# Exponentials and side counts one turn away from VectorE's work on them, in a fused attention and feed-forward kernel with a top-64 softmax

## What is computed

```python
q, k, v = (x @ W reshaped to 16 heads of 64)      # k and v get 4 memory rows in front
dots = einsum('bhid,bhjd->bhij', l2norm(q), l2norm(k)) * 10
dots = einsum('hg,bgij->bhij', W_pre_th, dots)     # mix the heads
dots = where(causal, -max, dots)
vk = top_k(dots, 64)[0][..., -1:]
attn = softmax(where(dots < vk, -max, dots))       # keep the 64 largest of a row
attn = einsum('hg,bgij->bhij', W_post_th, attn)    # mix the heads again
out = (attn @ v) * head_scale * sigmoid(x @ Wg + bg)
out = out @ Wo
```

## Time and profile before

| | |
|---|---|
| median of 3 runs | 3655.68 us (3652.28 to 3657.66) |
| the profiled execution's own time | 3655.08 us |
| span of its profile, first to last instruction | 3653.3 us |
| busy: PE, DVE, ACT, POOL | 2599.6, 1887.3, 1875.9, 1442.4 us |
| share of the span | 71%, 52%, 51%, 39% |
| mean granted TensorE clock | 0.795 of 2.4 GHz |

### The profile page before, as it was taken

The page is one execution under the profiler, slowest core; times in us unless marked ns, Lnnn a source line. Parts: engine busy times, 40 slices in busy tenths (PEclk is TensorE's granted clock), DMA queues, the critical chain, the costliest instruction groups (busy, mean ns, idle before and its releaser), DMA issues. The chain is left out here.

```text
span 3653.3 us, 58885 instructions
## 1 busy us (share of the span) xinstructions
PE 2599.6 (71%) x16099; PEld 1681.3 (46%) x16100; DVE 1887.3 (52%) x7291; ACT 1875.9 (51%) x6078; POOL 1442.4 (39%) x3918
## 2 busy tenths in 40 slices
PE   1985777777777776767677777676777777766498
PEld 1433444544454445544454445443544455444333
DVE  4262555545563556355545555455645563567335
ACT  1433555555654555455545554556545554565143
POOL 2003544444344444454444444544444335443000
PEclk9997777777877777877787777778877877787599
DMA  3001011001010111011101010011001010111101
GB/s 112 0 17 42 19 33 45 10 22 34 22 26 19 29 36 28 16 28 39 26 13 31 23 44 11 22 34 45 10 22 33 20 28 16 28 38 26 54 0 46
DMA packets 112976, 104.77 MB, mean 29 GB/s; under 512 B 34192, under 2 KB 110608, under 8 KB 112656
## 3 DMA queue, kind: packets, MB, share of 16 engines
q1 hardware_dynamic: 107744, 96.64, 10.4%
q10 hardware_dynamic: 4912, 4.46, 0.4%
HBM read 19.13 MB, written 12.71 MB: 9 GB/s over the span
## 5 line engine op out<-in xcount | busy, mean ns | idle before, releaser
L1395 DVE SCALAR_TENSOR_TENSOR E<-S,limit,E 128x68 f32<-128x68 f32 (+56 forms) x456 | 248.8, 579 | 1099.9 <-ACT E L1077 1074.3
L859 PE MATMUL bankC<-R,E 128*128 128x128 f32 x2560 | 475.4, 340 | 414.7 <-POOL R L1228 414.4
L859 PEld LDWEIGHTS bankC<-R,E 128*128 128x128 f32 x2560 | 415.0, 240 | 523.5 <-POOL R L1228 500.4
L1087 ACT COPY PT<-bankC 128x512 f32<-128x512 f32 (+3 forms) x512 | 216.5, 424 | 594.4 <-PE bankC L859 586.3
L1217 POOL TENSOR_SCALAR est<-below 128x1 f32<-128x1 f32 x456 | 93.2, 205 | 1029.0 <-ACT junk L1061 1007.7
L835 PE MATMUL bankD<-KT,QT 64*64 64x258 f32 (+7 forms) x2304 | 236.1, 485 | 353.2 <-ACT SC L1036 319.4
L845 PE MATMUL bankB<-raw,mixpre 128*128 128x76 f32 (+37 forms) x1024 | 417.7, 497 | 6.3 <-DMA raw<-SC 5.4
L1069 ACT ACTIVATE junk<-S 128x68 bf16<-128x68 f32 (+56 forms) x456 | 199.7, 439 | 432.3 <-DVE S L1333 432.0
L884 PE MATMUL bankM<-PT,V 128*64 128x64 f32 x5120 | 311.7, 292 | 0.8 <-ACT PTtail L1092 0.8
L845 PEld LDWEIGHTS bankB<-raw,mixpre 128*128 128x128 f32 x1024 | 187.6, 220 | 207.0 <-issue 188.0
L1189 POOL TENSOR_TENSOR S<-S,diagmask 128x8 f32<-128x8 f32 x512 | 127.3, 255 | 389.8 <-ACT S L1050 324.2
(11 more groups left out here) (173 smaller groups left out, 5428.5 us busy)
## 6 DMA issues: line engine op xcount, KB each, us to landing
X_first<-in_L_attn_x_dram ACTq DMA_DIRECT2D x8, 512.0 KB, 10.1
x<-X_first SPq DMA_DIRECT2D x8, 512.0 KB, 4.7
xt<-x SPq DMA_DIRECT2D x32, 128.0 KB, 3.2
x<-xt SPq DMA_DIRECT2D x32, 128.0 KB, 2.5
X_last<-x SPq DMA_DIRECT2D x8, 512.0 KB, 6.7
out_dram<-X_last SPq DMA_DIRECT2D x8, 512.0 KB, 3.2
raw<-SC SPq DMA_DIRECT2D x8, 258.0 KB, 4.5
raw<-SC SPq DMA_DIRECT2D x8, 254.0 KB, 4.1
```

The lines of the kernel that those rows point to most:

```text
L859: last = nc.tensor.matmul(bankC[n % 2][:, jb * P:(jb + 1) * P], E[n % 4][:, jb * P:(jb + 1) * P], R[n % 2][:, :], start=True, stop=True)
L1087: last = nc.scalar.copy(PT[u % 2][:, 0:blocks, :, at:at + IG], bankC[n % 2][:, 0:blocks * P].rearrange("p (j h i) -> p j h i", h=H, i=IG))
L1395: at[n] = step(nc.vector.scalar_tensor_tensor(out=E[n % 4][:, 0:w], in0=S[n % SBUFS][:, 0:w], scalar=least, in1=E[n % 4][:, 0:w], op0=ALU. ...
```

## The change

What moves: exp and count_sides of a pair both stand in ACT turn p+4 (before: turns p+6 and p+2), side counts first, and both behind the second evict of the turn; the two out_PT now follow each other. The waits of ACT are adapted. On POOL nmax comes first in the turn, then scaled_mix, then second_threshold. DVE shifts and takes the maxima of the pair four groups ahead instead of two, after the second round of 8 largest instead of between the rounds; the first four maxima are taken before the loop; ln_stats moves one turn earlier, and the squares of k one turn later. Instructions and buffers are the same in number and size.

```diff
--- before.py
+++ after.py
@@ -1043,6 +1043,8 @@
                 if is_ranked(n):
                     if ranked_upto(n - 2):
                         act.wait_ge(below_done, ranked_upto(n - 2))
+                    if ranked_upto(n - 6):
+                        act.wait_ge(signs_done, ranked_upto(n - 6))
                     nc.scalar.activation(junk[n % 2][:, 0:wide(n)], src, ACT.Square, scale=wide(n) ** -0.5,
                                          accum_out=msq[:, col(n)]).then_inc(summed, 1)
                     if is_wide(n):
@@ -1054,8 +1056,8 @@
 
             def count_below(n):
                 act.wait_ge(thr0_ready, ranked_upto(n))
-                if ranked_upto(n - 2):
-                    act.wait_ge(signs_done, ranked_upto(n - 2))
+                if ranked_upto(n - 4):
+                    act.wait_ge(signs_done, ranked_upto(n - 4))
                 act.wait_ge(summed, ranked_upto(n))
                 w = group_width(n)
                 nc.scalar.activation(junk[n % 2][:, 0:w], S[n % SBUFS][:, 0:w], ACT.Sign, scale=-1.0,
@@ -1063,8 +1065,10 @@
 
             def count_sides(n):
                 act.wait_ge(shifted, ranked_upto(n))
-                act.wait_ge(summed, ranked_upto(min(n + 2, NG - 1)))
-                act.wait_ge(below_done, ranked_upto(n))
+                if ranked_upto(n - 2):
+                    act.wait_ge(signs_done, ranked_upto(n - 2))
+                act.wait_ge(summed, ranked_upto(min(n + 4, NG - 1)))
+                act.wait_ge(below_done, ranked_upto(min(n + 2, NG - 1)))
                 w = group_width(n)
                 nc.scalar.activation(junk[n % 2][:, 0:w], S[n % SBUFS][:, 0:w], ACT.Sign,
                                      accum_out=signs[:, col(n)]).then_inc(signs_done, 1)
@@ -1126,16 +1130,15 @@
                         score(2 * t + 2, 1)
                     if g == 14 and ahead:
                         score(2 * t + 2, 3)
-                for n in (n0 - 6, n0 - 5):
+                if live:
+                    evict(n0 + 1)
+                for n in ranked_in(n0 - 4):
+                    count_sides(n)
+                for n in (n0 - 4, n0 - 3):
                     if 0 <= n < NG:
                         exp(n)
-                if live:
-                    evict(n0 + 1)
                 if n0 >= LAG:
                     out_PT(n0 - LAG)
-                for n in ranked_in(n0 - 2):
-                    count_sides(n)
-                if n0 >= LAG:
                     out_PT(n0 + 1 - LAG)
                 if live:
                     if g == 0 and ahead:
@@ -1236,21 +1239,21 @@
             for n0 in range(0, NG + LAG, 2):
                 t, g = divmod(n0, GPT)
                 live, ahead = n0 < NG, t + 1 < NT
-                if ranked_in(n0 - 2):
-                    second_threshold(ranked_in(n0 - 2))
+                if 0 <= n0 - 4 < NG:
+                    m = n0 - 4
+                    pool.wait_ge(max_done, m + 2)
+                    nc.gpsimd.tensor_scalar(nmax[:, ring((m, m + 1))], rmax[:, ring((m, m + 1))], -1.0, 1.0, ALU.mult,
+                                            ALU.mult).then_inc(nmax_ready, 2)
                 if n0 >= LAG:
                     scaled_mix(n0 - LAG)
                     scaled_mix(n0 + 1 - LAG)
+                if ranked_in(n0 - 2):
+                    second_threshold(ranked_in(n0 - 2))
                 if live:
                     mask(n0)
                     mask(n0 + 1)
                     if ranked_in(n0):
                         first_threshold(ranked_in(n0))
-                if 0 <= n0 - 4 < NG:
-                    m = n0 - 4
-                    pool.wait_ge(max_done, m + 2)
-                    nc.gpsimd.tensor_scalar(nmax[:, ring((m, m + 1))], rmax[:, ring((m, m + 1))], -1.0, 1.0, ALU.mult,
-                                            ALU.mult).then_inc(nmax_ready, 2)
                 for m in (n0 - 4, n0 - 3):
                     if 0 <= m < NG and m % GPB < 4:
                         if m >= 4:
@@ -1358,8 +1361,6 @@
                     for n in ranked:
                         dve.wait_ge(tk, at[n])
                         at[n] = step(nc.vector.max(top[n % 2][:, 0:8], near[n % 2][:, 0:group_width(n)]))
-                for n in ranked_in(n0 + 2):
-                    shift(n)
                 for r in range(1, WINDOW // 8):
                     for n in ranked:
                         row = near[n % 2][:, 0:group_width(n)]
@@ -1369,8 +1370,10 @@
                     for n in ranked:
                         dve.wait_ge(tk, at[n])
                         at[n] = step(nc.vector.max(top[n % 2][:, 8 * r:8 * r + 8], near[n % 2][:, 0:group_width(n)]))
-                if n0 + 2 < NG:
-                    for n in (n0 + 2, n0 + 3):
+                for n in ranked_in(n0 + 4):
+                    shift(n)
+                if n0 + 4 < NG:
+                    for n in (n0 + 4, n0 + 5):
                         row_max(n, ranked_upto(n))
                 if ranked:
                     for n in ranked:
@@ -1416,13 +1419,13 @@
             squares(0, 1)
             ln_stats(1)
             ln_apply(1)
-            for n in range(2):
+            for n in range(4):
                 row_max(n, 0)
             squares(1, 0)
             squares(1, 1)
             for n0 in range(0, NG, 2):
                 t, g = divmod(n0, GPT)
-                if g == 6 and t + 2 < NT:
+                if g == 4 and t + 2 < NT:
                     ln_stats(t + 2)
                 select_pair(n0)
                 if g == 4 and t:
@@ -1436,8 +1439,8 @@
                     if t + 2 < NT:
                         squares(t + 2, 0)
                     gate_half(2 * t)
-                if g == 14 and t + 2 < NT:
-                    squares(t + 2, 1)
+                if g == 0 and t and t + 1 < NT:
+                    squares(t + 1, 1)
                 if (n0 + 2) % GPB == 0:
                     mark_batch(n0 // GPB)
             gate_half(NU - 1)
```

## The result

The changed kernel takes 3053.23 us (median of 4 runs, 3052.16 to 3055.15) where the one before takes 3654.57: ratio 0.8355, 95% interval 0.834 to 0.8369. That is 601 us less, against a forecast of 380, and under the range's low end of 3140. The profiled execution took 3052.43 us, its span is 3050.7.

What follows compares the result with a forecast made beforehand. Bound: DVE and ACT waiting for each other, PE behind them. A tile of 80.8 + 21.7 = 102.5 us, for 116.2, scaled to 380 us off the attention: 3655.1 to 3275 us, range 3140 to 3500.

Steps and rivals of the forecast that it cites:

- The ring is opened: DVE and ACT wait for each other, 11.36 us a turn; becomes a two-turn loop, neither waiting in a plain turn.
- PE's wait for R: PE waiting for POOL's R at L859, 414.4 us before: should fall to the turns g = 8, under 200 us.
- I apply this share to the attention as a whole: 0.445 of one tile's PE idle time goes; applied to the attention's 860.6 us: 383 us, less 3 at the start.
- rival C: The clock rises too: busy PE shrinks by 216 us, two thirds of it on the path, 3131 us; chance 0.12.
- A: The attention as summed, with the waits of DVE and ACT opened: 3275 us, own range 3150 to 3420; chance 0.54.
- B: The ring is replaced by one through POOL (counts below, thr, shift, mask E, R, turn): 3515 us; chance 0.24.
- Handoffs at 1.3 us a turn: PE and ACT alternating over bankD and turned/out_PT: one 1.3 us handoff in each of seven turns, together 80.8 us.
- The turn g = 8: Turn with attend: R at 5.5 us, norm 1.1 us later, tail 16.0; 21.7 us for 22.44, bounds 20.2 and 22.4.
- waits and moves that cost nothing: ACT's new waits, POOL's nmax first, ln_stats earlier: covered or hidden; only the early maxima cost 3 us, once.
- Rival D: Exp stands behind both turn calls in ACT while R stays late: slower by 130 us, 3785; chance 0.05.
- exp behind turned: In ACT, exp waits for PE turn calls behind attend or project: 0.5 us in turns g = 0, 8 and 12.
- PE's wait for bankD: PE waiting until ACT has emptied bankD, 319.4 us before the change: should shrink least.

Runs made afterwards that it cites:

- the first experiment: Idle-time matmuls added ahead of the first turn call in turns g = 8: 14 on the kernel before, 3503.14 us; 10 on the kernel after, 2946.70 us.
- Q: POOL's new order (nmax, R, then second threshold): alone on the kernel before, 3470.97 us; the kernel after with it undone, 3583.01 us.
- X: Exponentials a turn earlier, behind the second evict: alone on the kernel before, 3699.41 us; the kernel after with it undone, 3042.22 us.
- a_norm8: The kernel after, with POOL's normalisation of k moved from the end of its turn g = 6 to the end of g = 8: 2933.93 us.

## Why the prediction was wrong

**The ring is opened: right in kind and in size.** I said PE would be left some 480 us idle in the attention; it is 482.9. ACT's wait before the side counts is gone, DVE waits at the shift, ACT's new wait at exp came as named; PE's wait for R, 210.7 us, stayed just over the 200 that I had set. That the idle time came out so close is partly luck: the share that goes was taken from one tile as 0.445, and it is 15.1 of 30.8, or 0.49, in that tile and 368 of 850.7, or 0.43, in the attention.

**The step that failed** is the one on which the sum was made: "I apply this share to the attention as a whole", with PE's busy time left at what it was, 85.4 us in the tile and 2177.8 overall. It fell by 228 us, to 1946.0. With the 368 of idle time that is 596 of the 601 us; the sum had put the busy time's part at nothing, without a price. I had that mechanism as rival C at 0.12, as another way to go, instead of a second term of the same sum. The sign for C, busy PE shrinking by more than 100 us, came, and the signs for A came with it.

C put the shrinking at 216 us for a clock of 0.90 and let two thirds of it count; it was 228 at 0.85, and all 228 stand beside the idle time in the 596. That C's 144 is near the 151 of the first experiment is chance, since these lie in the turns g = 8 and the gain of the change in the others. My argument against C, that a turn full of attend has the lowest clock and keeps it, was true of the change, at 0.60 before and after, but says nothing of the other turns, where the lower level went. Nor does that turn have to keep it: attend ran at 292 ns with a wait of 6 to 7 us ahead of it, and at 242 once that was filled. The Trainium skill says (TensorE: Matmul & The Clock Gate, "What's actually happening") that activity releases the throttle; the first experiment agrees with it.

One reading under C was wrong. The turn with 0.91 in the earlier trace rows is not one in which PE hardly waited: it was idle for 4.3 of 12.5 us. The turns g = 12 and g = 6 there, with 0.3 and 0.7 us idle, have 0.74 and 0.67. The clock of a turn does not follow from PE's idle time in the same turn. Under B, DVE is busy 9.3 to 10.2 us at g = 2 and 8 only, and 9.07 and 5.52 at g = 4 and 6.

**Handoffs at 1.3 us a turn** held as a sum in this tile. The seven turns took 71.8 us instead of 80.8, but the larger busy time of each is now 7.43, 8.36, 10.86, 9.86, 8.24, 9.37 and 7.68, together 61.8 instead of 71.7. That leaves 10.0 us for seven turns, 1.4 each. But the single turns leave from 0.3 to 2.8 us, so it is a mean and not one handoff in each. What it was added to was not right.

**The turn g = 8** I put at 21.7 us for 22.44, hardly a gain. It took 16.9 in the tile shown, which is not what such turns do: a sequence earlier it is 19.91 for 21.56, and the mean of all 32 fell by 0.9 us. The forecast was nearly right for the attention and wrong for its own tile. There, norm starts at 2112.95, 0.6 us before the turn, and R comes at 2118.09:

```profile
2112.95 3.02 POOL L1182 TENSOR_TENSOR rn<-ssq,neghalf 128x16 f32<-128x16 f32 x1
2113.52 0.66 ACT L1063 ACTIVATE junk<-S,thr 128x444 bf16<-128x444 f32 x1
...
2118.09 0.72 POOL L1231 TENSOR_SCALAR R<-mixpost,rinv 128x128 f32<-128x128 f32 x2
...
2118.51 1.82 PE L859 MATMUL bankC<-R,E 128*128 128x128 f32 x8 [3.87 <-POOL R L1231]
```

R is 4.6 us into the turn (I took 5.5): norm begins 0.2 us later against the turn than before, not 1.1. The tail from R to the turn's end is 12.4 us where I had kept 16.0, at a clock of 0.90 instead of 0.57. Why this turn has 0.90, and five of the eight in the same place of their sequence 0.60 to 0.67, stays open.

**POOL's new order** I filed under waits and moves that cost nothing, with 2 us of use at g = 8. As a cost that was right, and as a benefit it was not seen: the forecast took the ring as opened by the other moves, and without POOL's order 530 us of the gain stay away. The sum was right by taking all parts together; the account of which part does it was not. Rival B had the right suspicion, a ring through POOL, but the one that the runs show goes through mask and nmax, and only in the kernel without Q. Rival D fell with the time itself, and exp behind turned is part of X, which costs 11 us in all.

**PE's wait for bankD** was to shrink least; it halved, 319.4 to 153.8 us, a little more than the wait for R. That ACT no longer stood before its side counts while PE waited cannot be the whole reason: with X alone ACT does not stand there either (it waits 740.0 us for nmax, before exp), and PE's wait for bankD is 354.9 us. The cause was not tried by itself.

## What to carry to other kernels

When a change removes waits ahead of TensorE, put its busy time into the sum as well as its idle time: here that was 228 of 601 us. The durations of the same matmuls at either clock level stand in the trace of before; how many will change level was not known ahead, and their mean hides where it happens, so look at the clock turn by turn and in more than one tile. In engines that work strictly in order, look for the instruction that is ready but stands behind one that waits: moving it cost nothing here and was worth up to 599 us. And try parts of a rescheduling in all combinations, since here one part was worth 184 us alone and 599 beside another, and another part was worth nothing or less.

## What was not expected of the hardware

Adding matmuls made the kernel faster: 14 in each of 31 turns (868 records, two each), 195.0 us of busy time, took 151 us off, and 10 in each took 107 off the changed kernel. On a_norm8, at g = 6, where PE stands idle for 2.6 us a turn, 8 in each cost 55. With the first two the granted clock rose from 0.78 to 0.85 and from 0.85 to 0.93 in the attention, and the attend matmuls went from 292 to 242 and from 268 to 231 ns.
